# A GRU step in which h is formed as u + z*h and r's product is taken in two parts, with PSUM banks dealt out anew

## The reference

```
hh = h_rnn @ W_hh.T + b_hh            # 128 -> 3*128, split into h_r, h_z, h_n
r = sigmoid(i_r + h_r)                # i_* = W_ih product of the position
z = sigmoid(i_z + h_z)
n = tanh(i_n + r * h_n)
h_rnn = (1 - z) * n + z * h_rnn
h_ssm = silu(h_ssm @ A.T + bxt)       # 64 wide, beside it
```

## Time and profile before

| what | value |
|---|---|
| median of 3 runs | 738.71 us (737.09 to 740.52) |
| the profiled execution | 738.57 us, span 736.4 us |
| TensorE busy | 705.5 us (96%), 12892 instructions |
| VectorE busy | 443.7 us (60%), 2715 |
| ScalarE busy | 422.3 us (57%), 2689 |
| GpSimd busy | 128.4 us (17%), 219 |
| mean granted TensorE clock | 0.997 |

### The profile page before, as it was taken

The page is one execution under the profiler, slowest core; times in us unless marked ns, Lnnn a source line. Parts: engine busy times, 40 slices in busy tenths (PEclk is TensorE's granted clock), DMA queues, the critical chain, the costliest instruction groups (busy, mean ns, idle before and its releaser), DMA issues.

```text
span 736.4 us, 33392 instructions
## 1 busy us (share of the span) xinstructions
PE 705.5 (96%) x12892; PEld 532.1 (72%) x12892; DVE 443.7 (60%) x2715; ACT 422.3 (57%) x2689; POOL 128.4 (17%) x219
## 2 busy tenths in 40 slices
PE   8999999999999999999999999999999999999796
PEld 4677676667777777677777777777777777777685
DVE  6455555565665656666666666666666666667455
ACT  6655555556666555566666555666566656655332
POOL 2001111111110111111111111111111112222332
PEclk9999999999999999999999999999999999999999
DMA  8914000605422000063221001632210253322751
GB/s 309 349 65 177 6 6 7 234 6 182 153 90 84 14 13 14 13 218 134 92 89 57 20 14 34 244 116 77 86 54 17 89 200 99 100 96 95 285 166 51
DMA packets 45455, 76.55 MB, mean 104 GB/s; under 512 B 6284, under 2 KB 27090, under 8 KB 45170
## 3 DMA queue, kind: packets, MB, share of 16 engines
q1 hardware_dynamic: 41058, 68.40, 26.2%
q0 software_dynamic: 2368, 4.85, 2.3%
q10 hardware_dynamic: 1872, 1.18, 0.6%
HBM read 14.31 MB, written 21.04 MB: 48 GB/s over the span
## 4 chain that ended last, share of the span: by engine, by line
PE 81%; DVE 7%; ACT 4%; issue 3%; DMA 2%; SPq 0%; POOL 0%; DVEq 0%; POOLq 0%
PE nr_bank L1124 24%; PE s_bank L1124 24%; PE hid_bank_b L1124 9%; PE work L1124 7%; PE z_bank L1124 6%; PE y_bank L1124 6%; PE hid_bank_a L1124 5%; ACT r_fac L687 3%; DVE nr_bank L1017 3%; DMA xs_sb<-rows,x_index 2%; DVE s_ring L1021 1%; DVE fin_g L1101 1%; DVE hid_b L1083 1%; DVE o_sb L1105 1%; ACT h_ring L711 0%
## 5 line engine op out<-in xcount | busy, mean ns | idle before, releaser
L687 ACT ACTIVATE r_fac<-nr_bank 128x8 f32<-128x8 f32 x512 | 91.6, 179 | 248.4 <-PE nr_bank L1124 247.3
L1124 PE MATMUL s_bank<-s_ring,ws_sb 128*64 128x128 f32 x2048 | 221.2, 293 | 9.8 <-DVE s_ring L1021 2.4
L1124 PEld LDWEIGHTS nr_bank<-h_ring,w_sb 128*64 128x64 f32 x4096 | 167.4, 136 | 74.5 <-DVE h_ring L1025 71.7
L1124 PE MATMUL nr_bank<-h_ring,w_sb 128*64 128x16 f32 (+1 forms) x4096 | 213.5, 219 | 0.4 <-DVE h_ring L1025 0.2
L1017 DVE TENSOR_TENSOR_SCAN nr_bank<-r_fac,nr_bank 128x16 f32<-128x16 f32 x512 | 99.9, 195 | 157.3 <-ACT r_fac L687 152.9
L1124 PEld LDWEIGHTS s_bank<-s_ring,ws_sb 128*64 128x64 f32 x2048 | 106.9, 135 | 84.2 <-DVE s_ring L1021 53.9
L1025 DVE TENSOR_TENSOR_SCAN h_ring<-z_fac,h_ring 128x24 f32<-128x24 f32 x512 | 106.6, 208 | 97.0 <-ACT h_ring L711 96.0
L1124 PE MATMUL z_bank<-h_ring,w_sb 128*64 128x16 f32 x2048 | 142.5, 209 | 0.0
L1124 PEld LDWEIGHTS z_bank<-h_ring,w_sb 128*64 128x64 f32 x2048 | 106.2, 138 | 0.0
L711 ACT ACTIVATE h_ring<-nr_bank 128x16 f32<-128x16 f32 x512 | 95.5, 187 | 15.0 <-DVE nr_bank L1017 3.3
L709 ACT ACTIVATE z_fac<-z_bank 128x8 f32<-128x8 f32 x512 | 91.4, 179 | 1.0 <-PE z_bank L1124 0.5
(11 more groups left out here) (179 smaller groups left out, 958.2 us busy)
## 6 DMA issues: line engine op xcount, KB each, us to landing
wx<-w_all SPq DMA_DIRECT2D x66, 578.0 KB, 3.4
rows<-zeros SPq DMA_DIRECT2D x3, 4096.0 KB, 14.4
w_all<-in_w SPq DMA_DIRECT2D x2, 2048.0 KB, 15.7
xs_sb<-rows SPq DMA_DIRECT2D x54, 64.0 KB, 2.6
rows<-y_sb SPq DMA_DIRECT2D x54, 64.0 KB, 1.8
x_sb<-in_x SPq DMA_DIRECT2D x1, 1920.0 KB, 9.5
out<-o_sb SPq DMA_DIRECT2D x20, 64.0 KB
y_rows<-y_sb SPq DMA_DIRECT2D x12, 64.0 KB, 2.3
```

Of the source, the lines that this page charges most:

```text
L687: nc.scalar.activation(r_fac[:, t % 2, :, 1], r_cols(q, t), ACT.Sigmoid).then_inc(rn_ready, 1)
L1124: last = nc.tensor.matmul(out[c:c + COLS], weights[:, c:c + COLS], moving, start=start, stop=stop, skip_group_check=skip_group_check)
```

## The change

- The state is formed in three operations of 128x8 on VectorE. ScalarE gives v = 1 - z as sigmoid(-x). mw = (v - 1)*h_old is made before the tanh is waited for, u = v*n behind it, and h = u - mw behind u. `h_ring` is a plain 128x8 per step.
- r's product is taken in two parts that add up in PSUM: with -W_hr (negated once on GpSimd) and mw, as the last thing of the step before (`carried`), and with W_hr and u, as the first thing of the step. n and z wait for h.
- Moving operands of r, n and z are 8 columns wide; the state-space product has 64 weight columns.
- Banks: `nz_bank[q]` holds the n pairs of its own tile and the z sums of the other; `rs_bank[q]` the r and s sums of its own. The input products of n (t = 8) and z (t = 13) are made in `work` and copied with their bias by ScalarE; those of r (t = 11) and s (t = 12) are added in place. All stand in `tile_work`, in the middle of the step.
- On ScalarE every relu, copy and seed comes behind the tanh. `h_hist` and its copy go: TensorE reads `h_ring`.

```diff
 (VectorE, step)
+                    ge(eng, sig_ready, g + 1)
+                    ge(eng, h_ready, g)
+                    nc.vector.scalar_tensor_tensor(out=mw[:, k, :], in0=v_fac[:, k, :], scalar=1.0,
+                                                   in1=h_ring[:, pq, pt, :], op0=ALU.subtract,
+                                                   op1=ALU.mult).then_inc(mw_ready, 1)
                     ge(eng, tanh_ready, g + 1)
-                    nc.vector.tensor_tensor_scan(h_ring[:, q, t, 0:3 * B],
-                                                 z_fac[:, k, :, :].rearrange("p b m -> p (b m)"),
-                                                 scan_data(pq, pt), 0.0, ALU.mult, ALU.add).then_inc(h_ready, 1)
+                    nc.vector.tensor_tensor(u[:, k, :], v_fac[:, k, :], n_fac[:, k, :], ALU.mult).then_inc(u_ready, 1)
+                    ge(eng, mw_ready, g + 1)
+                    ge(eng, u_ready, g + 1)
+                    nc.vector.tensor_tensor(h_ring[:, q, t, :], u[:, k, :], mw[:, k, :],
+                                            ALU.subtract).then_inc(h_ready, 1)
...
 (TensorE)
+            def carried(g):
+                q, t = g // T % 2, g % T
+                if g == 1:
+                    eng.wait_ge(wr_negated, 1)
+                ge(eng, mw_ready, g)
+                mm(r_cols(q, t), wr_neg[:, :], mw[:, (g - 1) % 2, :], start=False, stop=True, skip_group_check=True)
...
 (TensorE, step)
+                    ge(eng, u_ready, g)
+                    mm(r_cols(q, t), w_sb[:, W_HH:W_HH + P], u[:, k, :],
+                       start=False, stop=True, skip_group_check=True).then_inc(r_ready, 1)
                     ge(eng, h_ready, g)
-                    mm(r_cols(q, t, R_WIDE), w_sb[:, W_HH:W_HH + P], h[:, 0:R_WIDE],
-                       start=False, stop=True, skip_group_check=True).then_inc(r_ready, 1)
-                    mm(n_pairs(q, t, N_WIDE)[:, :, 0], w_sb[:, W_HH + 2 * P:W_HH + 3 * P], h[:, 0:N_WIDE],
+                    if t == 14 and exists(c + 1):
+                        ge(eng, z_seeded, c + 2)
+                    mm(n_pairs(q, t)[:, :, 0], w_sb[:, W_HH + 2 * P:W_HH + 3 * P], h_ring[:, pq, pt, :],
                        start=False, stop=True, skip_group_check=True).then_inc(rn_ready, 1)
...
                     ge(eng, hs_ready, g)
-                    if t == 13 and exists(c + 1):
-                        pre(c + 1, 1 - q, 4)
                     state_space(g, pq, pt).then_inc(s_ready, 1)
-                if exists(c + 1):
-                    if t == 11:
-                        ge(eng, tanh_ready, g + 1)
-                        pre(c + 1, 1 - q, 2)
-                    if t == 12:
-                        ge(eng, sig_ready, g + 1)
-                        pre(c + 1, 1 - q, 3)
+                    if exists((g + 1) // T):
+                        carried(g + 1)
...
 (TensorE, state_space)
-                return mm(s_cols(g, width=S_WIDE), ws_sb[:, 0:P], s_ring[:, pq, pt, :],
+                return mm(s_cols(g, S_WIDE), ws_sb[:, 0:SSM], s_ring[:, pq, pt, :],
...
 (ScalarE, step)
+                    nc.scalar.activation(v_fac[:, k, :], z_cols(q, t), ACT.Sigmoid, scale=-1.0).then_inc(sig_ready, 1)
                     ge(eng, pre_n_ready, g + 1)
-                    nc.scalar.activation(scan_data(pq, pt).rearrange("p (b m) -> p b m", m=3)[:, :, 0:3:2],
-                                         n_pairs(q, t)[:, :, 1:2].to_broadcast([P, B, 2]),
-                                         ACT.Tanh).then_inc(tanh_ready, 1)
+                    nc.scalar.activation(n_fac[:, k, :], n_pairs(q, t)[:, :, 1], ACT.Tanh).then_inc(tanh_ready, 1)
...
+                if exists(c + 1):
+                    if t == 1:
+                        seed_nh(1 - q)
+                    if t == 3:
+                        seed_r(1 - q)
+                    if t == 5:
+                        ge(eng, hs_ready, c * T)
+                        seed_s(1 - q)
+                    if t == 7:
+                        pre_transposed(c + 1, 1 - q)
+                    if t == 8:
+                        copy_ni(c + 1, 1 - q)
+                    if t == 13:
+                        copy_z(c + 1, 1 - q)
```

More of the change, by code:

```diff
@@ L34 @@
 COLS = 64
[L35 to L36 removed]
+S_WIDE = 128
 KB = 3
@@ L55 @@
 Y_S, Y_G, Y_R = 0, P, P + 2
-SEED_STEPS = 6
+SEED_STEPS = 4
 BIAS_STEPS = 9
@@ L683, in step @@
             def step(g, c, q, t):
-                pq, pt = (q, t - 1) if t else (1 - q, T - 1)
+                k = t % 2
                 if exists(c):
                     ge(eng, r_ready, g + 1)
-                    nc.scalar.activation(r_fac[:, t % 2, :, 1], r_cols(q, t),
-                                         ACT.Sigmoid).then_inc(rn_ready, 1)
+                    nc.scalar.activation(r_fac[:, k, :, 1], r_cols(q, t), ACT.Sigmoid).then_inc(rn_ready, 1)
                 if 0 < g <= NT * T:
                     ge(eng, s_ready, g)
[L691 to L698, removed]
+                    nc.scalar.activation(s_fac[0:SSM, :], s_cols(g - 1), ACT.Sigmoid).then_inc(s_fac_ready, 1)
+                if exists(c):
+                    ge(eng, z_ready, g + 1)
+                    nc.scalar.activation(v_fac[:, k, :], z_cols(q, t), ACT.Sigmoid, scale=-1.0).then_inc(sig_ready, 1)
+                    ge(eng, pre_n_ready, g + 1)
+                    nc.scalar.activation(n_fac[:, k, :], n_pairs(q, t)[:, :, 1], ACT.Tanh).then_inc(tanh_ready, 1)
+                for place, (kind, n, second) in enumerate(UNITS.get(g - 1, [])):
+                    if place > 0 and not second and kind in "XAC":
                         leave_psum(kind, n)
@@ L756, in _ @@
             eng.wait_ge(seed_step, SEED_STEPS)
-            ge(eng, mod_copied, 1)
-            seed_r(0)
             eng.wait_ge(mod_taken, 3)
-            for part in range(2):
-                seed_n_part(0, part)
+            seed_nh(0)
             pre_transposed(0, 0)
             eng.wait_ge(bank_filled, 3)
-            seed_z(0)
-            eng.wait_ge(bank_filled, 4)
+            seed_r(0)
             seed_s(0)
+            copy_ni(0, 0)
+            copy_z(0, 0)
             steps(step)
@@ L1121, in mm @@
             def mm(out, weights, moving, start, stop, skip_group_check=False):
-                for c in range(0, P, COLS):
+                for c in range(0, weights.shape[1], COLS):
                     last = nc.tensor.matmul(out[c:c + COLS], weights[:, c:c + COLS], moving, start=start, stop=stop,
@@ L1136, in _ @@
             eng.wait_ge(zeros_set, 1)
-            fill(nr_bank[0])
-            fill(nr_bank[1])
+            fill(nz_bank[0])
+            fill(nz_bank[1])
             eng.wait_ge(ct_ready, 1)
@@ L1255, in tile_work @@
                     if t == 1:
-                        ge(eng, h_hist_ready, c)
-                        mm(work[:, Y_R:Y_R + P], h_hist[:, :], w_sb[:, W_PROJ:W_PROJ + P],
+                        ge(eng, h_ready, c * T)
+                        mm(work[:, Y_R:Y_R + P], h_ring[:, jq, :, :].rearrange("p t b -> p (t b)"), w_sb[:, W_PROJ:W_PROJ + P],
                            start=False, stop=False)
```

188 lines of the change are left out of this document (86 added, 102 removed).

## The result

The changed kernel takes 761.6 us in the median of three runs (760.5 to 763.1), the kernel before 738.7: 1.031 of it, with a 95% interval of 1.026 to 1.036. It is 3.1% slower, where I had forecast 725 and a range up to 751.

The account below looks back on a forecast made before the run. The prediction took a latency chain of five operations, 1.27 us a step, to bound the kernel. It summed 738.6 - 25.6 - 4.7 + 13.7 + 3.0 = 725 us, range 703 to 751, the forecast's own 716 to 734.

Parts of the forecast that it names:

- What bounds the kernel: Recurrence steps: a latency chain of five operations, 1.27 us in an ordinary step, sets the time; TensorE is not the limit.
- h = u - mw starts 0.03 behind u (the gap between the tanh and the h scan): VectorE, behind u: h ends at 0.20, n's product is seen at 0.60 against 0.61 for r's sigmoid; cost zero.
- rival B: Chain: u held back by mw, or n seen at 0.65, not 0.60; step 1.27, time 751; chance 0.16.
- Its other condition: VectorE: mw stands in front of u, which can start only when mw has ended, at 1.10.
- The chain: From u to the next u: 1.22 a step, a gain of 0.05 in each of 512 steps, -25.6 us.
- Side work on VectorE: Tile work starts 0.20 later against the chain; 114 steps without room lose 0.12 each: +13.7 us, bounds 0 and +23.
- 13.7 + 3.0 - 4.7: Terms of the sum: VectorE side work +13.7, ScalarE copies and relus behind the tanh +3.0, extras removed -4.7 us.
- the 114 scans: VectorE: steps outside the 398 with idle time before the scan, taken to have none; each loses between 0 and 0.20.
- Removed extras: Input products at t = 11 to 13 and a seed copy at t = 5 no longer delay the chain: -4.7 us.
- the copy of i_z at t = 14: ScalarE: the n product waits for this copy from the step before, about 0.1 in half of the tiles.
- Rival C: TensorE's clock falls to 1.2 GHz, 0.7 us more a step; 40 such steps cost 28 us: 753; chance 0.08.
- The Trainium skill's rule: VectorE: the next operation waits until the pipeline has emptied, so minimize operations; cited for the rival of 751, against observed starts.

Follow-up runs that it names:

- e4: The kernel before with only 8-column moving operands for r, n and z and 64 state-space weight columns: 733.9 us, 0.995 of the kernel before.
- e8: The kernel before with an always-satisfied z sigmoid wait added in front of the h scan, ahead of the tanh's wait: 767.2 us, 1.039.
- e1: The changed kernel with the two waits before h = u - mw in the other order, u first: 729.4 us, 0.989 of the kernel before.
- e3: e1 without the split of r's product, which takes h whole, with no product with mw: 810.2 us.
- e10: e1 with two extra 128x8 products of zeros behind h on VectorE, which nobody waits for: 761.5 us, 1.033 of the kernel before.
- e9: The kernel before with an always-satisfied z sigmoid wait added in front of the h scan, behind the tanh's wait: 739.0 us, 1.001.

## Why the prediction was wrong

**What bounds the kernel** was right. A latency chain set the step, TensorE's 96% didn't: taking two of its instructions away and narrowing others gave 0.01 a step (e4), while 0.07 on the chain moved all 512 (e8).

**The step that failed** is "h = u - mw starts 0.03 behind u (the gap between the tanh and the h scan)". I took the gap of an instruction with one wait for one with two, and did not look which of the two waits would be separate. It was 0.10. By my own count n's product then is seen at 0.67 and not 0.60, past the 0.61 of r's sigmoid (the scan started at 0.66), and the chain loses the 0.05 that it had won. With this step alone put right, in e1, the time is 729.4 and inside my range. This is rival B, by its second condition ("n is seen at 0.65 and not at 0.60"), to which I gave 0.16. Its other condition, mw holding u back, didn't occur: in the step above mw started at 309.98 and ran until 310.14, and u could start at 310.09, 0.03 behind the tanh, as in 503 of the 512 steps. I had noted that n's product had 0.01 to spare and that each 0.01 beyond costs 5 us. With so thin a margin the chance of B should have been near the forecast's.

**The chain.** With the waits turned round it is what I had drawn: 1.21 measured, 1.22 forecast, and 0.01 of it from the narrowing, which I had put at nothing. Product u, the tanh of 8 columns, the 0.39 to r's sigmoid and the half product ahead of u all have their forecast lengths. That the split's value is the distance from u to h is shown by e3.

**Side work on VectorE** was right in place and too small, and the sum around it was too. In e1 the 511 intervals sum to 650.9 us, 33 above 511 x 1.209. Before they sum to 658.1, 11 above 511 x 1.267. The difference, 22 us, stands against 13.7 + 3.0 - 4.7 = 12 in my sum for side work, ScalarE and removed extras. Of the 22, 17 lie in intervals whose scan VectorE's queue released (21.8 for 4.6), where I had 13.7 with an upper bound of 23. The other 5 (11.3 for 6.1), where I had -1.7, lie mostly in the intervals ending at t = 5, 7 and 10; what delays those wasn't tried. In the changed kernel itself the shift was 0.27 and not 0.20, as h's late start delays all behind it; 24 us of its excess over its median interval lie in intervals released by VectorE's queue. So B's 751 was 10 short of 761.6.

The count behind the 13.7 was misread. I took the 114 scans without a row among the 398 for scans without idle time. The view leaves out idle times up to 0.15 us: 57 of the 114 had some, and only 41 were held by the queue. Measured from the moment at which the queue would have let the scan start, 111 scans came less than 0.20 later, and what they lack of 0.20 adds up to 12.5 us. That the term came out near this was luck.

**Removed extras.** The intervals ending at t = 12, 13 and 14 were 1.30, 1.29 and 1.29 before; in e1 they are 1.25, 1.25 and 1.23, against an ordinary 1.21. Against the ordinary step they are no shorter than before, so this part of the -4.7 didn't come. Of the 3.4 us by which they exceed it in the whole run, 2.3 lie in the 19 intervals whose scan VectorE's queue released; for the copy of i_z at t = 14 at most 0.3 is left, where I had 0.1 in half of the tiles.

**Clock.** Rival C didn't occur: 1.00 in all the steps, also in e4. No run has a step at the lower clock, so the 0.7 a step that I had put on it stays an estimate.

**The Trainium skill's rule.** VectorE: DVE Perf Modes, section The DRAIN you can't avoid, says that the next operation does not start until the pipeline is empty. The same section adds that a next operation that is not held starts earlier, which I had left out, so the page gives rival B less support than I wrote. The traces agree with that addition: in the changed kernel the scan of 308.39 starts before the operation in front ends at 308.47. The advice to minimize the number of operations stands in another section of the page, Rules for kernel authors, and does hold here, for the reason that the queue's room is finite (e10). The section on the DRAIN also says that a semaphore after each of eight copies cost nothing extra against one after the last. No run here makes that comparison; what e1 and e8 show is 0.07 for a late second wait.

## What to carry to other kernels

Where a VectorE instruction on the critical chain waits for two things, see to it that the wait which ends last is the one that the instruction carries; in both places tried here (h of the changed kernel, the h scan of the one before) that is the one written first, and the profile shows the other order as a gap of 0.10 where one wait has 0.03. When a chain is shortened by making three operations out of one, cost two things apart: the new chain with every gap, and how much later the side work on that engine now starts, step by step and not by the mean idle time, nor by a count of idle times that leaves the short ones out. If a forecast rests on a margin of 0.01 us in each of 512 steps, give the other outcome the weight of a coin.

## What the runs showed of the hardware that I had not expected

A separate wait instruction in front of a VectorE operation adds 0.066 to 0.070 us to the hand-over when it ends last, and nothing measurable when it ends early (e9: 739.0 against 737.7, an interval that holds no change). Narrowing the moving operands of r, n and z to 8 columns and the state-space product to 64 weight columns made the ordinary interval 0.01 shorter (e4). And the same two 128x8 operations on VectorE cost 6 us in one kernel and 32 us in another, by how much room their step had left.
